# Graph attention on one core: the projection of later chunks in fp16 pairs, and a new order of the chunk loop

## What is computed

```
h   = maximum(layernorm(x), 0)                 # x: 8 x 2048 x 256
Wh  = h @ W                                    # W: 256 x 256
f1, f2 = Wh @ a[:256], Wh @ a[256:]
e   = leaky(f1[:, :, None] + f2[:, None, :])   # slope 0.2 below zero
e   = where(adj > 0, e, -9e15)
att = softmax(e, axis=1)                       # over the first node index
out = x + elu(att @ Wh)
```

## Time and profile before

| | |
|---|---|
| median of 3 runs | 1017.28 us (1016.97 to 1017.41) |
| the profiled execution | 1018.6 us, of which the span of the trace is 1016.8 us |
| granted TensorE clock, mean | 0.995 of full speed |
| busy: PE / PEld / DVE / ACT / POOL | 955.8 / 832.9 / 909.7 / 932.1 / 568.0 us |

### The profile page before, as it was taken

The page is one execution under the profiler, slowest core; times in us unless marked ns, Lnnn a source line. Parts: engine busy times, 40 slices in busy tenths (PEclk is TensorE's granted clock), DMA queues, the critical chain, the costliest instruction groups (busy, mean ns, idle before and its releaser), DMA issues.

```text
span 1016.8 us, 23983 instructions
## 1 busy us (share of the span) xinstructions
PE 955.8 (94%) x8989; PEld 832.9 (82%) x8989; DVE 909.7 (89%) x1261; ACT 932.1 (92%) x1472; POOL 568.0 (56%) x574
## 2 busy tenths in 40 slices
PE   8778999999999999999999999999999999899996
PEld 6556888888888888888888888888888888778786
DVE  7699988999989999899989999899998998899863
ACT  3699999999999999999999999999999999998973
POOL 5455454665645656655556556466564564655543
PEclk9899999999999999999999999999999999999999
DMA  9476567678858767767866876876785876777424
GB/s 221 81 114 105 94 100 131 123 133 141 134 113 150 131 125 130 134 130 135 150 114 123 148 133 119 140 131 127 138 146 110 152 111 106 128 115 125 67 64 141
DMA packets 190998, 127.45 MB, mean 125 GB/s; under 512 B 6434, under 2 KB 186914, under 8 KB 190883
## 3 DMA queue, kind: packets, MB, share of 16 engines
q0 software_dynamic: 132096, 67.11, 51.1%
q1 hardware_dynamic: 58786, 58.81, 18.7%
HBM read 176.16 MB, written 16.84 MB: 190 GB/s over the span
## 4 chain that ended last, share of the span: by engine, by line
POOL 48%; issue 45%; DMA 3%; ACT 1%; PE 1%; POOLq 1%; SPq 1%; DVE 0%; ACTq 0%; DVEq 0%
POOL direct L783 19%; POOL inv L780 7%; POOL raw L769 7%; POOL y L802 7%; POOL rstd L790 4%; POOL small_total L777 3%; DMA out<-y 1%; DMA f_scratch<-f_t 1%; ACT prob L501 1%; PE acc L347 1%; POOLq L228 0%; DMA prob<-in_W 0%; DMA f_row<-f_scratch 0%; DMA y<-in_x 0%; SPq L299 0%
## 5 line engine op out<-in xcount | busy, mean ns | idle before, releaser
L435 PE MATMUL acc<-v,direct 128*128 128x256 f16 x1024 | 279.3, 273 | 17.5 <-ACT z_direct L542 10.8
L673 DVE CUSTOM_DVE_ANT_0 prob<-tp,f_row 128x2048 f32<-128x2048 bf16 x128 | 291.9, 2280 | 3.7 <-DMA f_row<-f_scratch 3.6
L439 PE MATMUL acc<-v,direct 128*128 128x256 f16 x1024 | 279.2, 273 | 0.0
L437 PE MATMUL acc<-v,direct 128*128 128x256 f16 x1024 | 279.1, 273 | 0.0
L418 PE MATMUL acc_st<-v,stored 128*128 128x256 f16 x992 | 270.4, 273 | 0.0
L417 PE MATMUL acc_st<-v,stored 128*128 128x256 f16 x992 | 270.4, 273 | 0.0
L419 PE MATMUL acc_st<-v,stored 128*128 128x256 f16 x992 | 270.4, 273 | 0.0
L508 ACT ACTIVATE prob<-prob,shift 128x2048 f32<-128x2048 f32 x128 | 256.6, 2005 | 10.5
L501 ACT ACTIVATE prob<-prob,f 128x2048 f32<-128x2048 f32 x128 | 255.7, 1998 | 0.0
L777 POOL TENSOR_SCALAR small_total<-total 128x1 f32<-128x1 f32 x128 | 33.0, 258 | 387.2 <-ACT prob L508 387.2
L783 POOL TENSOR_TENSOR direct<-prob,inv 128x1024 f16<-128x1024 f32 x128 | 242.3, 1893 | 10.0
(11 more groups left out here) (84 smaller groups left out, 1361.2 us busy)
## 6 DMA issues: line engine op xcount, KB each, us to landing
raw<-in_adj POOLq DMA_DIRECT2D x64, 1024.0 KB, 9.3
y<-in_x SPq DMA_DIRECT2D x64, 256.0 KB, 2.9
out<-y SPq DMA_DIRECT2D x64, 256.0 KB, 2.4
x_in<-in_x SPq DMA_DIRECT2D x108, 128.0 KB, 3.0
f_row<-f_scratch SPq DMA_DIRECT2D x31, 256.0 KB, 3.5
stored<-in_x SPq DMA_DIRECT2D x4, 512.0 KB, 7.2
f_scratch<-f_t SPq DMA_DIRECT2D x124, 0.5 KB
stored<-in_x SPq DMA_DIRECT2D x4, 128.0 KB, 2.1
```

Of the source, the lines that this page charges most:

```text
L435: nc.tensor.matmul(acc[:, m, :], p_d[:, 0, rows], v_c[:, 0, :], start=(j == 0 and m % 2 == 0), stop=False, skip_group_check=True)
L437: nc.tensor.matmul(acc[:, m, :], p_d[:, 0, rows], v_c[:, 1, :], start=False, stop=False, skip_group_check=True)
L439: last = nc.tensor.matmul(acc[:, m, :], p_d[:, 1, rows], v_c[:, 0, :], start=False, stop=(j == C - 1), skip_group_check=True)
L673: nc.vector.tensor_tensor_reduce(out=prob[:, c % 2, :], in0=tp_b, in1=f1_row[:, b % 2, :], scale=1.0, scalar=-3.0e38, op0=ALU.add, op1=ALU ...
```

## The change

- **The product in fp16.** For chunks from 17 on, h is written by ACT as fp16 (`h_t[:, 0]`), and a new DVE operation `split_h_low` writes what is left over as a second fp16 number. W is split once in the same way. PE then runs six fp16 matmuls of 258 columns (high by high, high by low, low by high, for two halves of the 256 features) instead of two fp32 products. The columns W@a are scaled by the largest |a| so that they fit fp16, and `take_f` multiplies by the factor `k_f` (a value for each partition), so that the plain copy becomes an activation with a scale from memory. `w_cat` moves to memory that is used later for other things.
- **The order on PE** becomes `store_block`, `transpose_mask`, `make_wh`, `direct_blocks`, `transpose_x`. `direct_blocks` first runs the 16 matmuls that need only the high half, then waits for the low half and runs the other 8.
- **The order on ACT** becomes `make_h` of chunk s + 17 ahead of `attention`; then the leaky ReLUs; then `take_direct`'s second half, `keep_part`, `take_f` and `split_v_high`; then the shift and the exponential; then the ReLU of a finished pair, `normalise`, the pair's exponential, `split_high_stored`.
- **The order on DVE** becomes `mask_scores`, `split_h_low`, statistics, `add_halves` (of the same step's block), `split_low`, `split_v_low`, `turn_f1`, `make_offset`, `make_mask`, elu.
- **The sum with x** for the first 56 of 64 pairs is made by a DMA that POOL issues and that adds while it writes, instead of an addition on POOL; SP and ACT wait for that DMA where they waited for the addition.
- **f1's row:** SP reads a piece back after it has written the next one, but for the pieces that end a batch and for piece 2. W is loaded second instead of last among the first loads, and its largest value is found earlier.

```diff
+            def make_wh_split(c):
+                pe.wait_ge(h_low, c - LEAD + 1)
...
+                terms = [(h_part, w_part, k) for h_part, w_part in ((0, 0), (0, 1), (1, 0)) for k in range(KC)]
+                for i, (h_part, w_part, k) in enumerate(terms):
+                    last = nc.tensor.matmul(wh_bank(c)[:, 0:FW], h_t[:, h_part, k, :], w_split[:, w_part, k, :],
+                                            start=(i == 0), stop=(i == len(terms) - 1))
+                last.then_inc(wh_ps, 1)
...
-                pe.wait_ge(lo_direct, c + 1)
+                pe.wait_ge(hi_direct, c + 1)
...
+                pe.wait_ge(lo_direct, c + 1)
+                for m in range(NB):
+                    rows = slice(m * P, (m + 1) * P)
                     last = nc.tensor.matmul(acc[:, m, :], p_d[:, 1, rows], v_c[:, 0, :],
...
-                nc.scalar.copy(f12[:, i:j + 1:j - i], wh_bank(c)[:, FO:FW]).then_inc(f_ready, 1)
+                if c < LEAD:
+                    nc.scalar.copy(f12[:, i:j + 1:j - i], wh_bank(c)[:, FO:FW]).then_inc(f_ready, 1)
+                else:
+                    nc.scalar.activation(f12[:, i:j + 1:j - i], wh_bank(c)[:, FO:FW], ACT.Copy, scale=k_f
+                                         ).then_inc(f_ready, 1)
...
                 if chunk(s + LEAD):
+                    make_h(s + LEAD)
+                if chunk(s):
+                    leaky_scores(s)
+                if batch_over:
+                    take_direct((s - 1) // C - 1, 1)
+                n = block_at(s)
+                if n is not None and first_half(n):
+                    keep_part(n)
+                if chunk(s + LEAD):
                     take_f(s + LEAD)
                     split_v_high(s + LEAD)
                 if chunk(s):
-                    attention(s)
...
+                    exponentials(s)
...
+            def split_h_low(c):
+                dve.wait_ge(ht_ready, c + 1)
+                nc.vector.scalar_tensor_tensor(out=h_t[:, 1].rearrange("p k c -> p (k c)"), in0=xt_bank(c)[:, 0:F],
+                                               scalar=0.0, in1=h_t[:, 0].rearrange("p k c -> p (k c)"),
+                                               op0=ALU.max, op1=ALU.subtract).then_inc(h_low, 1)
...
+                if k < summed_by_dma:
+                    nc.gpsimd.dma_start(pair, elu[:, k % RE, :], accum_op=ALU.add).then_inc(y_sum[k % RY], 16)
+                    return
```

More of the change, by code:

```diff
@@ L73, in graph_attention @@
         xn = sb("xn", [P, 2, F], F32)
-        h_t = sb("h_t", [P, KC, P], F32)
+        h_t = sb("h_t", [P, 2, KC, P], F16)
         f12 = sb("f12", [P, 64 + RF], F32)
@@ L114, in graph_attention @@
         y_out = [sem(f"y_out{i}") for i in range(RY)]
-        f1_written = sem("f1_written")
+        f1_written = [sem(f"f1_written{i}") for i in range(2)]
         f1_row_in = [sem(f"f1_row_in{i}") for i in range(2)]
@@ L130, in graph_attention @@
         a_spread = sem("a_spread")
+        a_max = sem("a_max")
+        a_max_spread = sem("a_max_spread")
+        w_high = sem("w_high")
+        w_split_s = sem("w_split_s")
+        set_w = sem("set_w")
         w_ready = sem("w_ready")
@@ L158, in graph_attention @@
         y_ready = sem("y_ready")
+        y_sum = [sem(f"y_sum{i}") for i in range(RY)]
         stats_s = sem("stats_s")
@@ L189, in h_buf @@
         def h_buf(c):
-            return h_t_early[:, c % 2, :].rearrange("p (k c) -> p k c", k=KC) if c < LEAD else h_t[:]
+            return h_t_early[:, c % 2, :].rearrange("p (k c) -> p k c", k=KC) if c < LEAD else h_t[:, 0]
         def measured_at(s):
@@ L218, in pieces_sent, with read_alone @@
             return n - (1 if n > 3 else 0)
+        def read_alone(piece):
+            return piece == 2 or piece % 4 == 3 and piece > 3
         FIRST = -26
@@ L343, in make_wh @@
                     pe.wait_ge(w_scaled, 1)
-                if c < LEAD:
-                    wait(pe, v_ready, c - 3)
+                wait(pe, v_ready, c - 3)
                 for k in range(KC):
@@ L386, in spread_max_w, with spread_max_a @@
                 nc.tensor.matmul(max_all, ones, tops[0:1, 1:2], start=True, stop=True).then_inc(w_max_all, 1)
+            def spread_max_a():
+                pe.wait_ge(a_max, 1)
+                nc.tensor.matmul(a_max_all, ones, a_max_one, start=True, stop=True).then_inc(a_max_spread, 1)
             def spread_last_f1():
@@ L477, in scale_w, with split_w_high @@
                 nc.scalar.activation(w_nat, w_raw, ACT.Copy, scale=tops[:, 5:6]).then_inc(w_scaled, 1)
+            def split_w_high():
+                nc.scalar.activation(w_split[:, 0, :, 0:FO], w_raw, ACT.Copy, scale=tops[:, 5:6]).then_inc(w_high, 1)
             def take_f(c):
@@ L547, in finish_relu @@
                 b, i = finishing[k]
-                wait(act, y_ready, k - RE + 1)
+                wait_for_y(act, k - RE)
                 if i < 4:
@@ L575, in _ @@
                 if chunk(s):
-                    attention(s)
-                if batch_over:
-                    take_direct((s - 1) // C - 1, 1)
-                if chunk(s + LEAD + 1):
-                    make_h(s + LEAD + 1)
-                n = block_at(s)
-                if n is not None and first_half(n):
-                    keep_part(n)
+                    exponentials(s)
                 for k in finish(s):
@@ L616, in largest_of_all, with largest_a, split_w_low, after @@
                 nc.vector.reduce_max(tops[0:1, 1:2], max_t, AX_X).then_inc(w_max_one, 1)
+            def largest_a():
+                nc.vector.reduce_max(a_max_one, a_one, AX_X, apply_absolute_value=True).then_inc(a_max, 1)
+            def split_w_low():
+                steps = [0]
+                def after(ins):
+                    steps[0] += 1
+                    ins.then_inc(set_w, 1)
+                    dve.wait_ge(set_w, steps[0])
+                dve.wait_ge(w_high, 1)
+                nc.vector.scalar_tensor_tensor(out=w_split[:, 1, :, 0:FO], in0=w_raw, scalar=tops[:, 5:6],
+                                               in1=w_split[:, 0, :, 0:FO], op0=ALU.mult, op1=ALU.subtract
+                                               ).then_inc(w_split_s, 1)
+                dve.wait_ge(a_max_spread, 1)
+                after(nc.vector.tensor_scalar(tops[:, 6:7], a_max_all, 1e-30, None, ALU.max))
+                after(nc.vector.reciprocal(a_inv, tops[:, 6:7]))
+                after(nc.vector.tensor_scalar(k_f, tops[:, 2:3], tops[:, 6:7], 1.0 / W_TOP, ALU.mult, ALU.mult))
+                after(nc.vector.tensor_scalar(f_cols, w_cat[:, :, FO:FW], tops[:, 5:6], a_inv, ALU.mult, ALU.mult))
+                after(nc.vector.tensor_copy(w_split[:, 0, :, FO:FW], f_cols))
+                nc.vector.tensor_tensor(w_split[:, 1, :, FO:FW], f_cols, w_split[:, 0, :, FO:FW], ALU.subtract
+                                        ).then_inc(w_split_s, 1)
+            def split_h_low(c):
[3 more added lines that the diff above has]
+                                               op0=ALU.max, op1=ALU.subtract).then_inc(h_low, 1)
             def make_factors():
@@ L713, in _ @@
                     mask_scores(s)
-                n = block_at(s - 1)
-                if n is not None and not first_half(n):
-                    add_halves(n)
+                if chunk(s + LEAD) and s >= 0:
+                    split_h_low(s + LEAD)
                 for c in measured_at(s):
@@ L727, in _ @@
                     split_v_low(LEAD - 1)
+                n = block_at(s)
+                if n is not None and not first_half(n):
+                    add_halves(n)
+                if chunk(s - 1):
+                    split_low(s - 1)
                 if chunk(s + LEAD) and s != -1:
```

94 lines of the change are left out of this document (64 added, 30 removed).

## The result

The changed kernel takes **1056.96 us** (median of 4 runs, 1055.73 to 1058.2), the kernel before, run beside it, 1017.12 us (1015.81 to 1017.41): a ratio of **1.0389, 95% interval 1.037 to 1.0408**. 1049 was forecast, 1035 to 1062 the range. The profiled execution's span is 1056.4 us, 39.6 longer than before.

A forecast was written before the change was run, and what follows sets the result against it. ACT, gapless in a batch's second half, was taken as the bound. Copy of f, `inv` waits and old gaps +20 (batches 1 to 6) and +6 (first), DVE +7, start and end -1: +32 on 1017.3, 1049 us, range 1035 to 1062.

The forecast's parts named there:

- the waits for `inv`: ACT before `stored`: 0.59 us idle in each step without a pair, 8 x 0.59 a batch.
- The copy of f: On ACT's path: 0.15 us more for each of 111 chunks, 16.7 us, taking `most` as the same form.
- The DVE term: Steps 4, 6 and 8, elu meeting `add_halves`: scores late by 0 to 0.6 us, 0.4 taken in 18 steps, +7.
- The sign I had named: In ACT's timeline, DVE's `top` as the releaser of `most` in steps 4, 6 and 8 would show the DVE term.
- The old gaps: ACT's 3.4 us of waits a batch in steps 0 to 7, mostly around the batch's turn: all go.
- A batch by its terms: ACT's work and waits: 116.8 + 16 x 0.15 + 8 x 0.59 = 123.9 us against 120.7, +3.2.
- the forecast's 27 us for six batches: Batches 1 to 6: +20 from copy of f, waits for `inv` and old gaps, and +7 from DVE.
- Start and end: Six small DVE operations more, W sooner: -1 us, between -2 and +2.
- PE counted at nothing: Projection on PE: six fp16 matmuls save 0.23 x 111 = 25 us, counted at nothing because gapless ACT covers PE.
- "has time to spare": PE in the kernel before waits 23.1 us in the run for DVE's `top`, so it has slack where ACT has none.
- The DMA that adds at nothing: Additions of x by DMA: about 1 us of issue under POOL's idle time; cost 0, up to +5 if delaying a load.
- the fourth: Rival: DVE binds in every step with an elu and `add_halves`, 18 x 0.6 = 11, DMA delays +5: 1058; 20%.

The follow-up runs named there:

- e_fcopy: Changed kernel with the copy of f for chunks from 17 on as a plain copy, factor `k_f` left out: 1050.41 us, ratio 1.0308.
- e_statslast2: Changed kernel with DVE's statistics moved to the end of its step and POOL's root of the variance taken one step later: 1058.66 us, ratio 1.038.
- e_h: Changed kernel with ACT's ReLU for the projection put back behind the exponential, `keep_part` left ahead of it: 1034.61 us, ratio 1.0146.
- e_pe8: Changed kernel with eight matmuls instead of six in each later chunk's projection, adding the product of the low halves: 1059.51 us, ratio 1.0397.
- v_bspread: Kernel before with 56 additions of x made by the DMA and each finished pair's exponential one step after its ReLU: 1032.66 us, ratio 1.0135.
- e_pooladd: Changed kernel with all 64 additions of x back on POOL instead of 56 by the DMA: 1061.03 us, ratio 1.0411.
- e_statslast: Changed kernel with DVE's statistics moved from the front of its step to the end, POOL's root not moved: 1087.76 us, ratio 1.0673.
- e_fill2: Changed kernel with ACT's ReLU for the projection and `keep_part` behind the exponential, PE's stored block behind the projection: 1421.77 us, ratio 1.4001.

## Why the prediction was right, and where its terms were off

- **The direction and its main cause** hold. ACT sets the pace, f's copy and the waits for `inv` come on top. Forecast was a wait of 0.59 us in each step without a pair and 75 waits in all; measured are 73 (51.5 us and not 40, as 27 of them are about 1 us long: 18 in steps 4, 6 and 8 of the six middle batches, nine from step 14 of the last but one batch on), and step 10 is 0.71 us longer, of which 0.10 is the copy and 0.61 the wait. Steps of 7.6 and 8.0 were forecast, 7.55 and 7.98 came; 7.22 in the first batch, 7.18 came.
- **The copy of f** was mis-sized: `most` was taken for the same form, and its 0.20 us start to start, less the old copy's 0.04, gave 0.15. But the new copy takes 0.14 to 0.15 in all; why `most` takes longer isn't shown. It costs 0.10 to 0.11 more than the old copy in the timeline, 0.09 in e_fcopy's steps: 10 to 12 us and not 16.7. The rows of `h_t` and `part` (0.36 and 0.46) had said it. The rule of the Trainium skill (ScalarE: Activation LUTs, What ACT_TABLE_LOAD costs), about 93 ns for a pointer operand, gave 10 us; the runs agree.
- **The DVE term** had the right cause and was too small: I took 0.4 us in 18 steps, +7. With the usual wait, a step without a pair and without `part` takes 7.18 (seven of the first nine steps of the first batch, 7.17 to 7.26); steps 4, 6 and 8 take 7.90, 7.78, 7.97: 2.1 us a batch, 12.7 us. The sign I had named, `top` releasing `most`, didn't show, because POOL's stretched sum held ACT back by the same amount; only e_statslast2 brought it out, and e_fcopy, whose steps 6 and 8 stay as long with less work on ACT. What I had overlooked is the tie in the other direction: in light steps DVE waits for ACT's ReLU (0.84 us at 582.03), so it can't work ahead for the heavy ones. e_h cuts the tie, and steps 6 and 8 fall to 6.92 and 6.91; step 4 keeps 0.6 us more (7.54).
- **The stretched sum** is a case of the rule I had cited for L687, the Trainium skill (SBUF — State Buffer, Who interferes with whom): the trace agrees with it, the other way round, since here GpSimd's small operation waits out VectorE's (0.22 to 0.78 us).
- **A batch by its terms:** 116.8 of ACT's work + 1.6 for f + 8 x 0.61 of waits + 2.1 of DVE = 125.4; batches 1, 3, 4 and 5 take 125.5 (forecast 123.9 + 1.2 = 125.1). That these are so near is in part luck: the copy of f was 0.8 us a batch too much, DVE 0.9 too little. The rest of the difference to the forecast's 27 us for six batches: in the kernel before, batches 5 and 6 took 120.07 and 119.37 and not 120.7 (2 us), and batch 2 of the changed kernel has two late steps (8.26 and 8.67, 1 us).
- **The old gaps** went, as forecast: ACT no longer waits for PE's projection. But they were misread as lying mostly around the turn of the batch. In batch 4 of the kernel before, that is one wait of 0.65 us; 2.0 us lie in steps 4 to 6 (`inv`, `top` and PE's projection).
- **Start and end** were forecast at -1, measured -0.6 and +1.0, and the last batch +1.5 where I had 0: 2.9 us of the 7.6 by which the sum fell short.
- **PE counted at nothing** was right for the changed kernel (e_pe8), and so was its step of 7.0 us there: start to start the pieces are 2.62 for each of the two groups of 24 matmuls, 0.89 for the mask, 0.67 for the projection and 0.22 for x, 7.02 in all, under steps of 7.55 and 7.98. That PE "has time to spare" in the kernel before holds only barely: with the fp32 projection its step is 7.23 (v_bspread), 0.12 to 0.14 under the mean step of batches' second halves.
- **The DMA that adds at nothing**: in the changed kernel nearly so (e_pooladd, 1.0411 against 1.0389, intervals overlap). As a change of its own it gains 0.5%. L785's mean is 1.28 us, near the 1.25 forecast for it. Of the rivals, the fourth (1058), in which DVE takes 0.6 us in these steps (0.7 measured), was nearest in time; its DMA part has no support.

What stays open: what a version would take that has both fillers back and x's transposes ahead again on PE, as in the kernel before. It wasn't tried.

## What to carry to other kernels

Where one engine waits for a short answer of another in each step, whatever stands in that gap is free, and whatever is moved out of it costs its full length where nothing else fills the gap, even if no work is added: one ReLU of 0.26 us, moved back, gave over 20 of the 40 us here, part of it because it also untied DVE from ACT. Three engines whose busy times lie within 4% of each other have no room for a trade: 0.23 us a step taken from PE bought nothing here, 0.10 more on ACT counted in most steps, and DVE with 0.34 more came late in three steps of a batch. Before an order is mended in one place, follow what each engine's first and last piece waits for once around the ring of all of them; e_statslast and e_fill2, which skipped that, cost 3% and 35% on top of the change.

## What the runs showed of the hardware

- A POOL operation on one element per partition took 0.56 to 0.87 us instead of 0.22 when a DVE operation with two SBUF inputs ran beside it (steps 3, 4, 6 and 8 of the changed kernel). Two inputs aren't needed: DVE's mask, which has one, did the same by itself in four steps of the last batch of the kernel before (0.53 to 0.55 us). So the mask may have a part in steps 4 and 8 too, where it lies over the sum's start.

```profile
925.92 0.53 POOL L777 TENSOR_SCALAR small_total<-total 128x1 f32<-128x1 f32 x1 [2.43 <-ACT prob L508]
```

```profile
925.69 0.68 DVE L661 TENSOR_SCALAR neg<-raw 128x2048 bf16<-128x2048 bf16 x1
```

- Two copies of the same two elements on ACT, one plain (COPY) and one with a scale from memory (ACTIVATE), differ by 0.10 us start to start (0.04 against 0.14 to 0.15).
- A DMA that adds 256 KB in SBUF costs POOL 0.93 us of issue (905 to 968 ns, 56 of them) and lands after 4.1 us (3.3 to 7.1). With it in the kernel before (e_before_dma) no step of a middle batch grew by more than 0.02 us (medians). In the changed kernel:

```profile
L909 POOL DMA_DIRECT2D y<-elu x56: 905/929/968, 189.3 to 1026.2; - x56
...
DMA to landing us min/median/max: 3.3/4.1/7.1
```
